# GpSimd makes three quarters of VectorE's source marks while the edge list is turned into matrices

## The reference, cut to what matters

```python
h = relu(layernorm(x)); x = x + gcn(h)        # A[src, dst] += edge_weight, two layers
h = relu(layernorm(x)); x = x + attention(h)  # 4 blocks, scores only where an edge is
h = relu(layernorm(x)); x = x + diffusion(h)  # 3 steps over the row-normalised 0/1 matrix
h = relu(layernorm(x)); x = x + rgcn(h)       # 2 relations, weights mixed from 30 bases
```

## Time and profile before

| what | us |
|---|---|
| median of 3 executions | 902.92 |
| lowest and highest | 899.2 and 903.7 |
| span of the profiled execution | 898.7 |
| TensorE busy | 842.5 |
| VectorE busy | 560.8 |
| ScalarE busy | 398.6 |
| GpSimd busy | 230.9 |

### The profile page before, as it was taken

One profiled execution on the slowest core, in us unless ns is written; L12 is line 12 of the kernel. 1 busy time (PEld: TensorE's weight loads), 2 busy tenths in 40 slices (PEclk: granted clock), 3 DMA queues, 4 the chain that ended last, 5 costly groups with the idle time before them and its releaser, 6 DMA issues. The chain is left out here.

```text
span 898.7 us, 13977 instructions
## 1 busy us (share of the span) xinstructions
PE 842.5 (94%) x4222; PEld 637.2 (71%) x4223; DVE 560.8 (62%) x1221; ACT 398.6 (44%) x646; POOL 230.9 (26%) x253
## 2 busy tenths in 40 slices
PE   4999789999789999999997999999999979799998
PEld 2666556767567778777694777877777857488786
DVE  6999987658956666477655575674766636620110
ACT  3999893234435612356223365134561325431210
POOL 4000022208512123401254022343212404413200
PEclk9999999999899999999998999999999989899999
DMA  7999924524245643537533346535366386130100
GB/s 169 201 215 238 271 49 128 155 76 128 94 117 119 181 107 115 138 99 193 133 114 90 97 98 189 132 118 135 86 183 156 106 225 173 31 94 0 47 12 35
DMA packets 37846, 113.39 MB, mean 126 GB/s; under 512 B 5908, under 2 KB 6472, under 8 KB 30108
## 3 DMA queue, kind: packets, MB, share of 16 engines
q1 hardware_dynamic: 20604, 79.00, 36.7%
q10 hardware_dynamic: 17184, 33.69, 10.9%
HBM read 105.33 MB, written 7.34 MB: 125 GB/s over the span
## 5 line engine op out<-in xcount | busy, mean ns | idle before, releaser
L690 POOL TENSOR_TENSOR wl<-wraw,wh 128x512 fp32r<-128x512 f32 x140 | 179.7, 1318 | 412.7 <-ACT wh L768 379.3
L1806 PE MATMUL ring<-ohs,ohd 128*128 128x512 f32 x312 | 79.7, 408 | 6.4 <-DVE ohs L1317 6.4
L1806 PEld LDWEIGHTS ring<-ohs,ohd 128*128 128x128 f32 x312 | 59.1, 194 | 31.3 <-issue 18.6
L1295 DVE SCALAR_TENSOR_TENSOR ohd<-iota,dstT,vals 128x256 fp32r x156 | 69.8, 481 | 7.9 <-PE ring L1806 4.5
L768 ACT ACTIVATE wh<-wraw 128x2048 fp32r<-128x2048 f32 x35 | 66.9, 1910 | 8.4 <-PE ring L1704 5.0
L793 ACT ACTIVATE yT_h<-ring 128x512 fp32r<-128x512 f32 x32 | 19.1, 597 | 99.6 <-PE ring L1722 99.6
L817 ACT ACTIVATE ohs<-iota,minus_srcT 128x512 fp32r<-128x512 f32 x78 | 52.4, 713 | 16.1 <-PE ring L1806 9.6
L1733 PE MATMUL mix_ps<-quad,att_shift 120*32 120x512 f32 x384 | 52.5, 623 | 7.4 <-DMA quad<-in_L_gnn_basis 7.4
L695 POOL TENSOR_TENSOR rstd<-ve,half 128x1 f32<-128x1 f32 x44 | 24.1, 551 | 105.3 <-DVE ve L1146 105.0
L1704 PE MATMUL ring<-yT_h,wh 128*128 128x512 f32 x128 | 49.8, 389 | 0.0
L1704 PE MATMUL ring<-yT_l,wh 128*128 128x512 f32 x128 | 49.8, 389 | 0.0
(11 more groups left out here) (382 smaller groups left out, 2159.8 us busy)
## 6 DMA issues: line engine op xcount, KB each, us to landing
quad<-in_L_gnn_basis SPq DMA_DIRECT2D x60, 960.0 KB, 8.0
wraw<-in_L_gnn_m_w ACTq DMA_DIRECT2D x8, 1024.0 KB, 6.0
mix_scratch<-mixed SPq DMA_DIRECT2D x128, 32.0 KB, 4.0
wraw<-in_L_gnn_wv ACTq DMA_DIRECT2D x4, 1024.0 KB, 5.3
wraw<-in_L_gnn_wq ACTq DMA_DIRECT2D x4, 1024.0 KB, 5.2
wraw<-in_L_gnn_wk ACTq DMA_DIRECT2D x4, 1024.0 KB, 5.4
wraw<-in_L_gnn_wo ACTq DMA_DIRECT2D x4, 1024.0 KB, 5.3
wraw<-mix_scratch ACTq DMA_DIRECT2D x4, 1024.0 KB, 5.7
```

What stands on the lines that cost most here:

```text
L690: last = g.tensor_tensor(wl[s][:, k, :], wraw[s][:, k, :], wh[s][:, k, :].bitcast(F32), ALU.subtract)
L1295: return v.scalar_tensor_tensor(out, at.unsqueeze(1).broadcast_to([P, 4, HALF]), dstT[:, e], vals[:, e, :].rearrange("p a b -> p (a b)").u ...
L1806: last = te.matmul(ring[:, banks[b], :], ohd[:, s, b, :], ohs[:, s, :], start=False, stop=False)
```

## The change

GpSimd makes the source marks of six of the eight edge tiles of VectorE in every word (`POOL_OF`: edge tile 2 in units 0 and 2, edge tiles 0 and 2 in units 1 and 3), in the first 32 units alone. For each, VectorE copies the column of `srcT` into `source_of` and GpSimd compares `iota` with it; TensorE waits for `pool_marks` there. ScalarE copies `iota` once into PSUM bank 4 (`node_nos`), and VectorE reads the node numbers there, in all 39 units, for the destination marks and its remaining source marks. SyncE issues the four `att` columns ahead of basis group 0. TensorE clears its second bank ahead of its first waits. GpSimd's small constants come after its 48 marks and after the roots of the layer norm.

```diff
+POOL_OF = ((2,), (0, 2), (2,), (0, 2))
+POOL_BEFORE = (0, 1, 3, 4)
+POOL_PER_WORD = 6
+MARK_BANK = 4
...
+        node_nos = ring[:, MARK_BANK, :]
...
-            load_pass_group(0, 0)
             for l in range(2):
                 for r in range(2):
                     sp.dma_start(att[0:QUADS * BASES, l, r:r + 1], ...).then_inc(att_loaded, 16)
-            for k in range(1, GROUPS):
+            for k in range(GROUPS):
                 load_pass_group(0, k)
...
+            pool.wait_ge(flags_ready, 1)
+            n = 0
+            for i in range(SURE):
+                for u in POOL_OF[i % WORD]:
+                    n += 1
+                    at = i % 2 * BODY + u
+                    pool.wait_ge(source_copied, n)
+                    g.tensor_scalar(ohs[:, at, :], iota[:], source_of[:, at:at + 1], None, ALU.is_equal).then_inc(pool_marks, 1)
+
+            def input_roots():
+                pool.wait_ge(ln_var, NT)
...
+            input_roots()
+            pool.wait_ge(ln_xn, NT)
             pool.wait_ge(cond_clear, 1)
             g.memset(quarter[FREQS:2 * FREQS, :], 0.25).then_inc(const_step, 1)
...
+            act.wait_ge(const_ready, 1)
+            act.wait_ge(tile_taken, pre.base + pre.at["tab"] + 1)
+            a.activation(node_nos, iota[:], ACT.Copy).then_inc(iota_banked, 1)
             act.wait_ge(flags_ready, 1)
+            act.wait_ge(iota_banked, 1)
...
-                at = iota[:, bass.ds(half * HALF, HALF)]
+                at = ring[:, MARK_BANK, bass.ds(half * HALF, HALF)]
...
-            def unit(i, j, word):
+            def unit(i, j, word, by_pool=()):
...
                     dve.wait_ge(onehot_used, i * BODY + (u + 1))
+                    if u in by_pool:
+                        v.tensor_copy(source_of[:, s:s + 1], srcT[:, e]).then_inc(source_copied, 1)
                     ins = destination(half, s, e)
-                    if u not in ACT_OF:
-                        ins = v.tensor_scalar(ohs[:, s, :], iota[:], srcT[:, e], None, ALU.is_equal)
+                    if u not in ACT_OF + by_pool:
+                        ins = v.tensor_scalar(ohs[:, s, :], node_nos, srcT[:, e], None, ALU.is_equal)
...
+                    if u in by_pool:
+                        pe.wait_ge(pool_marks, k * POOL_PER_WORD + (POOL_BEFORE[j] + POOL_OF[j].index(u) + 1))
...
             zero(0, True)
+            zero(1, True)
             pe.wait_ge(flags_ready, 1)
             pe.wait_ge(att_step, 3)
-            zero(1, True)
```

More of the change, by code:

```diff
@@ L249, in program @@
         vec_rows = sb("vec_rows", [VEC_ROWS, P], ctx=ec2)
-        sb("unused", [P, 640], ctx=ec2)
+        sb("unused", [P, 640 - SLOTS], ctx=ec2)
+        source_of = sb("source_of", [P, SLOTS], ctx=ec2)
         bias_raw = sb("bias_raw", [P, D], ctx=ec2)
@@ L349, in program @@
         distance_ready = sem("distance_ready")
+        iota_banked = sem("iota_banked")
+        source_copied = sem("source_copied")
+        pool_marks = sem("pool_marks")
         onehot_used = sem("onehot_used")
@@ L667, in _ @@
                             pattern=[[0, D]], channel_multiplier=1).then_inc(cond_clear, 1)
+            pool.wait_ge(flags_ready, 1)
[8 more added lines that the diff above has]
+                pool.wait_ge(ln_var, NT)
+                g.tensor_tensor(rstd[:], ve[:], half[:], ALU.pow).then_inc(ln_rstd, NT)
+                pool.wait_ge(ln_rstd, NT)
+                g.tensor_tensor(nmean[:], mv[:, :, 0], rstd[:], ALU.mult).then_inc(mean_step, 1)
+                pool.wait_ge(mean_step, 1)
+                g.tensor_scalar(nmean[:], nmean[:], -1.0, None, ALU.mult).then_inc(ln_xn, NT)
+            input_roots()
+            pool.wait_ge(ln_xn, NT)
             pool.wait_ge(cond_clear, 1)
@@ L1338, in _ @@
             dve.wait_ge(vals_ready, 1)
+            dve.wait_ge(iota_banked, 1)
             with dve.Fori(0, SURE // WORD) as k:
@@ L1342, in _ @@
                 for j in range(WORD):
-                    unit(k * WORD + j, j, word)
+                    unit(k * WORD + j, j, word, POOL_OF[j])
             dve.wait_ge(x_loaded, 16)
@@ L1783, in zero, with unit @@
                 return te.matmul(ring[:, at, :], zero_l[:], zeros, start=start, stop=not start)
-            def unit(i, j, word):
+            def unit(i, j, word, k, by_pool=()):
                 first = pe.snap((word >> (BITS * j + BITS - 1)) & 1)
@@ L1815, in later_units @@
                     with pe.If(count > k * WORD + j):
-                        unit(k * WORD + j, j, word)
+                        unit(k * WORD + j, j, word, k)
             def mix_in_units(m, k):
@@ L1838, in _ @@
                             mix_in_units(m, g * 2 + j // 2)
-                        unit(m * (2 * WORD) + (g * WORD + j), j, word)
+                        unit(m * (2 * WORD) + (g * WORD + j), j, word, m * 2 + g, POOL_OF[j])
             count = pe.value_load(words[0:1, WORDS:WORDS + 1])
```

6 lines of the change are left out of this document (removed).

## The result

The changed kernel took 907.75 us (median of 4, 903.81 to 909.52) against 901.49 for the kernel before in the same measurement: ratio 1.0068, interval [1.0047, 1.0089]. It is slower by about 6 us, outside the range; the forecast was 1.5 us faster.

What follows compares the result with a forecast made beforehand. TensorE was taken to pace the 32 units, VectorE the seven later ones. Terms -2.0 - 0.7 - 2.8 + 1.2 + 2.8 = -1.5 us took 902.9 to 901.4 us; range 896.5 to 907.5.

Steps and rivals of the forecast that it cites:

- It gets ahead of TensorE by up to eight slots, and the 0.7 us of stalls go: 32 units: VectorE, rid of 48 source marks for 48 one-element copies, runs ahead and stops delaying TensorE: -0.7 us.
- under the 32 units: GpSimd's 48 marks at 1.6 us take 77 us, from 13.6 to 90, hidden while the 32 units run to near 100.
- Columns first: Start: attention columns issued before the basis let TensorE begin 4.7 us earlier, but basis group 4 limits the gain to 2.0.
- SyncE issues the same list up to there: Start: basis group 4 comes through the same queue, so no reason for it to land earlier than 36.5.
- waits until 36.5: Fifth pair: TensorE would want basis group 4 at 33.9 and wait for its landing, gaining 2.1 us, taken as 2.0.
- Node numbers in PSUM: Seven later units: 14 source marks of VectorE pay 0.2 us each for the PSUM operand, +2.8 us.
- The destination mark's 0: VectorE's destination marks cost the same from PSUM as from SBUF: 0, ends 0 and 1.7 us in the later units.
- The gap at unit 32: TensorE's idle time after unit 31 falls from 5.2 to 2.4 us as VectorE comes ahead: -2.8, ends 0 and 4.
- Waits of TensorE: 32 units: 48 new waits on `pool_marks`, between 0 and 4.0 us, taken as +1.2 us.
- Contention: 32 units: GpSimd does not hold up VectorE, whose marks have one tensor in PSUM and one in SBUF: 0.
- copies held: Rival, 32 units: GpSimd holds VectorE's one-element copies some 0.8 us each, giving some 925 us; chance 0.05.
- GpSimd becomes the pace: Rival, 32 units: GpSimd's marks set the pace if each takes m over 1.79 us; 911.3 us at 2.0; chance 0.11.

Runs made afterwards that it cites:

- e5: The changed kernel with the old start (basis group 0 ahead of the attention columns, second clearing product behind the wait): ratio 1.0051 to the kernel before.
- e6: The changed kernel with the old start and each source column copied four units ahead, spread out, GpSimd waiting for its slot itself: ratio 1.0019 to the kernel before.
- e8: The changed kernel with the old start, source columns copied ahead spread out, and the later units' node numbers in SBUF: ratio 0.9982 to the kernel before.
- e12: The kernel of e8 timed once more, unchanged, in another measurement: ratio 0.9996 to the kernel before.
- e4: The changed kernel with all of VectorE's node numbers read from SBUF instead of PSUM: 912.74 us, one execution.
- e2: The kernel before with only the attention columns ahead of basis group 0 and the second clearing product ahead of the first waits: ratio 1.0032.
- e10: The kernel before with the four attention column transfers on ScalarE's DMA queue, behind its edge loads: ratio 1.0145.
- e1: The changed kernel with VectorE's node numbers read from SBUF again in the units after the thirty-second: ratio 1.0055 to the kernel before.
- e3: The changed kernel with all six source columns copied in one burst ahead of each copy-out, GpSimd waiting for its slot itself: ratio 1.0076 to the kernel before.

## Why the prediction was wrong

**The step that failed most** is "It gets ahead of TensorE by up to eight slots, and the 0.7 us of stalls go", with GpSimd's marks costed as 48 times 1.6 us "under the 32 units". I asked for GpSimd's throughput and got it right: 1.56 us, TensorE the pace up to 1.79. I did not ask when each column reaches it. The copies stand in VectorE's queue behind its wait for the closing product and its copy-out, GpSimd needs 1.54 us where VectorE needed 0.40, and so four pairs are late: +5.0 us instead of -0.7. Shown by e5 to e6: the same marks with early columns, 62.71 to 58.25 us in that stretch and 0.0032 in the time. The relief itself is worth nothing there: 58.3 to 58.6 us, no less than the 57.68 before.

**Columns first** (-2.0; ends 0 and -4.7). The step "SyncE issues the same list up to there" failed: the list is the same, the moment at which the first 960 KB start is not. Group 4 was issued at 23 us as before but landed 15.3 us later, at 38.3. The working stopped at "waits until 36.5"; the wait lasted until 38.3, so the fifth product gained the 0.3 us between this landing and the 38.60 at which TensorE had come to it before. By itself the edit costs 0.0032 on the kernel before and 0.0017 in the change, so the truth lay beyond the end that I had called 0.

**Node numbers in PSUM.** +2.8 for the later units was right in mechanism and small in size: from mark to next mark 0.66 us for 0.40, not 0.60, so 14 marks are 3.6. VectorE's stretch, from its first later mark to its last, grew by 3.5 (23.3 for 19.8). The whole stage grew by 4.3; the rest goes with a lower granted clock (0.88 for 0.92 in the two windows), which no run separates from it. The destination mark's 0 was right (475 ns for 479). What I did not see is that PSUM is also a help, to GpSimd's `att_shift`.

**The gap at unit 32** (-2.8). Right in sign, 1.33 measured. VectorE was free when the half was closed, as the working had it, and from there to its first mark went 5.93 us (103.29 to 109.22), the 6.0 of the working. But the half is closed 3.5 us before TensorE's end (103.29 to 106.78), not 4.7, which is 1.2 of the 1.5 missing; VectorE had waited 1.57 us for it. This, too, is a lead that a wait takes away. And the 1.33 is not the relief's alone: in e8 and e12, with the late pairs repaired, the idle time is 4.46 and 4.41, a gain of 0.7. That is what VectorE's relief is worth at this place, a quarter of the 2.8, and it is about what the stretch ahead of it loses (0.9).

**Waits of TensorE** (+1.2): 0 to be seen, quiet pairs 4.85 to 4.88. **Contention** (0) and **copies held** (rival): right, 144 ns each; e4 shows what the PSUM bank avoids. **GpSimd becomes the pace** (rival): not by price, yet by being late; it was the nearest of the four, and I had tied it to m > 1.79 us alone.

The remaining disagreement, open: the traces put the three causes at 8.4 us (136.28 to 127.83), the times at 7.7 us by e8 or 6.5 by e12. The start's share is 1.5 us by the changed kernel against e5 and 2.9 by e2; the intervals don't settle which.

## What to carry to other kernels

When work moves from a fast engine to a slow idle one, cost the delay from the moment at which its input is released to the moment at which its output is wanted, after every wait and copy-out in the releasing engine's queue; the sum of its busy times says only that it could keep up. Hand inputs over a whole round ahead, spread out. A first transfer that is large belongs ahead of small ones that are slow to issue, for the engines behind the queue idle meanwhile. And a cheap operand in one stage is a dear one where the same helper runs alone: choose the operand by stage.

## What was unexpected of the hardware

- Issuing a transfer of 0.5 KB took SyncE 0.83 to 1.07 us (mean 0.93 in e2) and ScalarE 0.86 to 1.69 us (mean 1.09 in e10), about what one of 960 KB took (0.84 to 1.07).
- A transfer of 0.5 KB on another queue landed only behind each 960 KB of the first one: 14.6 us from issue to landing (median of four), against 3.2 with nothing ahead of it and 6.7 behind one group.
- GpSimd's 120x19 mark with two pointers took 802 ns beside VectorE's marks from SBUF and 480 beside those from PSUM; its 128x512 mark 1896 and 1563 ns. VectorE's copy of one element was never held, 144 ns.
- In e1, e2 and e3 the pair behind TensorE's wait for group 4 (2.27, 2.79, 3.08 us) took 6.42, 6.42 and 7.55 us instead of 4.85, with the granted clock down; in the two profiles of the changed kernel (2.14, 1.84) it took 4.85.
- Behind the edge stage the same code took from 765.6 to 772.3 us in the fourteen profiles of the table, with the granted clock of the whole span between 0.970 and 0.981.
